# State reads of a gated delta-rule kernel on Trainium2: 64 columns in place of 128, with an overlapped layernorm, later loads and a loop body of four chunks

## The chip, the cores and the metric

The kernel is one program on one core of one Trainium2 chip. The metric is the device time of one launch in microseconds (us). TensorE (PE) runs its matmuls at one of two clock levels, 1.2 and 2.4 GHz; the profile writes the granted clock as 0.50 and 1.00 of full speed.

## The reference, cut to what matters

```python
xn = _layernorm(x, axis=-1)                      # x: (4, 512, 256)
def step(S, xs):                                 # per batch and head: 64 states S of 128x128
    q_t, k_t, v_t, a_t, b_t = xs
    Sk = einsum('bhvk,bhk->bhv', S, k_t)
    S = a_t[..., None] * S - (b_t[..., None] * (Sk - v_t))[..., None] * k_t[:, :, None, :]
    o_t = einsum('bhvk,bhk->bhv', S, q_t)
    return (S, o_t)
...
o = (o - mu) * lax.rsqrt(var + 1e-05) * ln_g + ln_b
return (o * g).reshape(B_, T_, H * DV) @ Wo.T
...
x = x + attention(xn) + ffn(xn)                  # ffn: router over 8 experts (top 2), LoRA on gate, up, down
```

q, k and v come from projections of xn, a causal convolution of four taps and a silu; the decays a and the weights beta come from sigmoids.

## The kernel before, in words

The five engines run hand-written queues; semaphores tie them together, and each engine takes its own queue in order. All tiles lie in one SBUF tile, `arena`, so nearly every row of the profile says arena; PSUM is `PS`, eight banks of 512 columns.

**Prelude (0 to 271 us).** x arrives in four quarters of 512 tokens. For each quarter VectorE (DVE) makes the layernorm in seven steps (lines 882 to 894: sum, mean, subtract, square, sum, reciprocal, multiply), with a square root on ScalarE (ACT, line 600) between them. TensorE transposes the quarter (line 1211), ACT copies it out (605, 608). When all four are done, TensorE computes the router logits (line 1219: 16 tiles of tokens, weights 128x128, 8 moving columns each), the beta projection (1225) and, after a chain of small DVE steps on the logits (909 to 927), transposes of the expert weights (1229). Then the FFN runs.

**Projections (271 to 740 us)** write q and k, k times beta, v, decays and suffix products to DRAM (`kq_d`, `kb_d`, `vas_d`, `e_d`), the last stores by SyncE's queue (SPq, lines 368 to 386).

**Start of the recurrence (738 to 790 us).** ACT issues the loads of the first two chunks (lines 700 to 702: KB, KQ, EX for chunk 0 and chunk 1), computes the first products, issues the loads of VAS (line 738, four slots), writes products to `r_d` and gathers them into `g_d` (732, 743), waits for the projections' stores, loads GB (748) and gives `x_read` (752), on which DVE's first step of chunk 0 (line 1051) waits.

**Recurrence (782 to about 2250 us).** 16 chunks of 32 tokens, each in 8 blocks (m) of 4 tokens, on 64 pairs of batch and head at once. DVE does the steps inside a block (1051 to 1074), takes off corrections from PSUM (1002, 1013), copies the block's last column of P (line 1114, the mark of a block's end used below), adds state updates (1019), extends decays (1025, 1030). TensorE turns P (1406) and makes the corrections (1418, 1335, weights of 32 rows). Beside that, in the blocks of `READ_AT`, it reads the states for the next chunk: 16 slots of 4 pairs per chunk. For a slot ACT scales four states (769), TensorE transposes them (1367), ACT copies them to `STR` (774), TensorE multiplies them with the next chunk's keys and queries (1379, `reads_of`), ACT copies the result into X (783). PSUM bank 6 holds the transposes and bank 7 the reads, one slot at a time. In between stand the update products (1393), the products for the next chunk (1303, 1325, `prep`), key transposes (1295) and, at the head of a chunk, three matmuls whose result nobody reads (1447, `keep_awake`).

A read multiplies each transposed state with the columns of two neighbouring pairs, its own and the other of the couple, 128 columns; the copy takes the half that belongs to its own pair:

```python
p0 = 4 * (g0 + gi) + j // 2 * 2
ins = mm(bank(7)[:, 128 * gi:128 * (gi + 1)]..., STR[:, s % 2, gi, :], KQ[d][:, :, p0:p0 + 2]...)
...
nc.scalar.copy(dst, bank(7).rearrange("v (g l o x) -> v o g l x", g=4, l=NB, o=2)[:, j % 2])
```

15 of the 16 chunks read, so there are 240 slots and 960 read matmuls; an fp32 matmul stands in the profile as two instructions, hence 1920. `chunks` runs the chunks in a loop whose body holds two of them (7 turns, chunks 0 to 13) and then chunks 14 and 15 alone.

**End (2250 to 2591 us).** Normalisation, gates and the output projection.

Of the kernel before, what the change touches and what calls it, by code (L numbers as in the profile page):

```python
# [28 lines left out]
HALO = KC - 1  # L29
# [70 lines left out]
def build(nc, x_tm, wqT, wkT, wvT, waT, wgT, woT, small, w_gate, w_up, w_down, a_gate, b_gate,  # L100
# [15 lines left out]
    with ExitStack() as ctx:  # L116
# [109 lines left out]
        XAG = take(CH)  # L226
        XAU = take(CH)
        SG = take(2 * CH).rearrange("p (s t) -> p s t", s=2)
        SQ = SG.rearrange("p s t -> p (s t)")
# [19 lines left out]
        ln_step, ln_var, ln_std, xn_ready = sem("ln_step"), sem("ln_var"), sem("ln_std"), sem("xn_ready")  # L249
# [345 lines left out]
        def _(act):  # L595

            act.wait_ge(consts, 7)
            for c in range(4):
# [3 lines left out]
                if c > 0:  # L602
                    for k in range(2):
                        act.wait_ge(xnT_psum, 2 * (c - 1) + k + 1)
                        nc.scalar.copy(XNT[:, k, c - 1, HALO:HALO + T], bank(2 * (c - 1) + k)).then_inc(xnT_ready, 1)
            for k in range(2):
                act.wait_ge(xnT_psum, 6 + k + 1)
                nc.scalar.copy(XNT[:, k, 3, HALO:HALO + T], bank(6 + k)).then_inc(xnT_ready, 1)
            act.wait_ge(logits, 1)
# [89 lines left out]
            for n in range(2):  # L699
                act.dma_start(KB[n].rearrange("k p t -> k (p t)"), kb_d[n:n + 1].rearrange("s k x -> k (s x)")).then_inc(kb_in[n], 16)  # L700
                act.dma_start(KQf[n], kq_d[n:n + 1].rearrange("s k x -> k (s x)")).then_inc(kq_in[n], 16)
                act.dma_start(EX[n].rearrange("v r p -> v (r p)"), e_d[n:n + 1].rearrange("s v x -> v (s x)")).then_inc(e_in[n], 16)

# [33 lines left out]
            for m in range(4):  # L737
                act.dma_start(VAS[:, m].rearrange("v r p t -> v (r p t)"), vas_d[:, m:m + 1].rearrange("v l r x -> v (l r x)")).then_inc(vas_in[m], 16)
# [21 lines left out]
            def chunk(n, i, c, nxt, nxt2):  # L760
# [15 lines left out]
                def read_copy(s):  # L776
# [6 lines left out]
                    nc.scalar.copy(dst, bank(7).rearrange("v (g l o x) -> v o g l x", g=4, l=NB, o=2)[:, j % 2]).then_inc(x_read, 1)  # L783
# [92 lines left out]
        def _(dve):  # L876
            tt = nc.vector.tensor_tensor

            for c in range(4):
                cs = slice(4 * c, 4 * c + 4)  # L880
                dve.wait_ge(ld_x[c], 16)
                nc.vector.tensor_reduce(ST8[:, 0, cs], XIN[:, cs, :], AX.X, ALU.add).then_inc(ln_step, 1)
                dve.wait_ge(ln_step, 5 * c + 1)
                nc.vector.tensor_scalar(ST8[:, 3, cs], ST8[:, 0, cs], -1.0 / D, None, ALU.mult).then_inc(ln_step, 1)
                dve.wait_ge(ln_step, 5 * c + 2)
                tt(XN[:, cs, :], XIN[:, cs, :], ST8[:, 3, cs].unsqueeze(2).to_broadcast([128, 4, D]), ALU.add).then_inc(ln_step, 1)
                dve.wait_ge(ln_step, 5 * c + 3)
# [315 lines left out]
        def _(pe):  # L1203
# [3 lines left out]
            for c in range(4):  # L1207
# [5 lines left out]

            pe.wait_ge(ld_small, 16)
            pe.wait_ge(xnT_ready, 8)
            for i in range(NX):
                at = HALO + 128 * (i % 4)
                for k in range(2):
                    ins = mm(bank(0)[:, E * i:E * (i + 1)], XNT[:, k, i // 4, at:at + 128], WR[:, k, :], start=(k == 0), stop=(k == 1))
            ins.then_inc(logits, 1)  # L1220
# [137 lines left out]
            def chunk(n, i, c, nxt, nxt2):  # L1358
# [11 lines left out]
                def reads_of(s):  # L1370
# [218 lines left out]
```

## Time and profile before

| | |
|---|---|
| median of 3 runs | 2592.14 us (2591.98 to 2592.34) |
| the profiled execution's own time | 2592.64 us |
| its span, first to last instruction | 2590.9 us |
| TensorE matmul busy | 2181.5 us (84%) |
| VectorE busy | 1925.3 us (74%) |
| ScalarE busy | 1276.5 us (49%) |
| mean granted TensorE clock | 0.912 |

The profiled execution's time is its span plus 1.7 us around it, and 0.5 us above the median of the runs. Busy shares are means over stages of different kinds, so stages and blocks are looked at one by one.

### The profile page before, as it was taken

What the parts mean: (1) busy time and instruction counts of PE and PEld (TensorE: products, weight loads), DVE (VectorE), ACT (ScalarE), POOL (GpSimd) and SP (SyncE); (2) the same over time, 40 slices, a digit from 0 to 9 for tenths busy, and PEclk for the clock granted to TensorE, in tenths of its full rate; (3) what the DMA queues carried; (4) which work ended last, traced back from release to release, by engine and by line L of the source; (5) the groups of instructions that cost most, each with busy time, mean ns of one, the idle gap of its engine ahead of it and who ended that gap; (6) DMA issues with size and microseconds to landing.
All of it is one profiled execution on the core that took longest, in us unless ns stands there. A gap on an engine that the chain in (4) does not pass through costs nothing.

```text
span 2590.9 us, 61369 instructions
## 1 busy us (share of the span) xinstructions
PE 2181.5 (84%) x21482; PEld 1606.6 (62%) x21482; DVE 1925.3 (74%) x4379; ACT 1276.5 (49%) x2731; POOL 578.6 (22%) x577
## 2 busy tenths in 40 slices
PE   5999999999948777778878878777878786799998
PEld 3444888888836666667666667666666665344343
DVE  5222799999968889888888888988887898633334
ACT  2000677777833555445445455554544543334443
POOL 0000244444442222122222222221222222200000
PEclk9999999999977898898898898888888988899999
DMA  6000277777684555555555555555555556310210
GB/s 244 8 8 8 101 277 266 266 265 268 237 328 148 200 180 196 165 189 183 170 196 176 182 176 183 202 166 190 184 165 196 178 193 216 144 66 16 81 67 23
DMA packets 211170, 434.65 MB, mean 168 GB/s; under 512 B 47153, under 2 KB 160553, under 8 KB 181721
## 3 DMA queue, kind: packets, MB, share of 16 engines
q1 hardware_dynamic: 207880, 420.24, 46.9%
q10 hardware_dynamic: 2976, 10.72, 1.0%
q8 instruction: 167, 2.74, 0.4%
q14 instruction: 99, 0.80, 0.1%
q0 software_dynamic: 48, 0.16, 0.0%
HBM read 295.13 MB, written 136.98 MB: 167 GB/s over the span
## 4 chain that ended last, share of the span: by engine, by line
PE 51%; DVE 22%; issue 13%; ACT 11%; SPq 1%; DVEq 1%; DMA 1%; ACTq 0%; POOL 0%; POOLq 0%
PE PS L1379 10%; DVE arena L968 8%; ACT arena L769 4%; PE PS L1520 4%; PE PS L1275 4%; PE PS L1325 3%; PE PS L1252 3%; PE PS L1418 3%; PE PS L1354 3%; PE PS L1367 3%; PE PS L1406 3%; DVE arena L1059 2%; DVE arena L1002 2%; PE PS L1506 2%; PE PS L1393 2%
## 5 line engine op out<-in xcount | busy, mean ns | idle before, releaser
L1275 PE MATMUL PS<-arena 128*128 x2048 | 463.6, 386 | 1.8 <-DVEq L953 0.9
L968 DVE SCALAR_TENSOR_TENSOR arena<-PS,SM,arena 128x256 f32<-128x256 f32 x1152 | 452.8, 474 | 15.5 <-ACT arena L648 15.5
L1275 PEld LDWEIGHTS PS<-arena 128*128 128x128 f32 x2048 | 383.4, 188 | 82.1 <-DVE arena L968 6.5
L1379 PE MATMUL PS<-arena 128*128 128x128 f32 x1920 | 332.3, 326 | 76.5 <-ACT arena L774 75.3
L1379 PEld LDWEIGHTS PS<-arena 128*128 128x128 f32 x1920 | 281.3, 225 | 119.4 <-ACT arena L774 93.7
L575 POOL TENSOR_TENSOR arena<-arena 128x256 f32<-128x256 f32 x128 | 114.7, 896 | 1062.2 <-DVE arena L1074 1062.2
L769 ACT ACTIVATE arena<-arena 128x128 f32<-128x128 f32 x960 | 302.0, 395 | 0.0
L648 ACT ACTIVATE arena<-PS,SM 128x256 f32<-128x256 f32 x384 | 209.8, 565 | 88.9 <-PE PS L1275 84.1
L783 ACT COPY arena<-PS 128x256 f32<-128x256 f32 x240 | 89.6, 373 | 267.1 <-PE PS L1379 266.2
L795 ACT COPY arena<-PS 128x512 f32<-128x512 f32 (+1 forms) x188 | 91.0, 520 | 263.0 <-PE PS L1406 262.7
L1367 PE MATMUL PS<-ident,arena 128*128 128x128 f32 x960 | 177.4, 316 | 27.0 <-ACT arena L769 25.2
L1393 PE MATMUL PS<-arena 32*128 32x128 f32 x1920 | 169.1, 324 | 31.8 <-issue 18.4
L1013 DVE TENSOR_TENSOR arena<-arena,PS 128x512 f32<-128x512 f32 x192 | 127.4, 684 | 86.8 <-PE PS L1418 84.4
L1051 DVE TENSOR_TENSOR arena<-arena 128x64 f32<-128x64 f32 x512 | 155.2, 303 | 43.1 <-issue 17.5
L1074 DVE TENSOR_TENSOR arena<-arena 128x384 f32<-128x384 f32 (+2 forms) x384 | 175.2, 456 | 13.8 <-DVE arena L1051 3.2
L543 POOL TENSOR_TENSOR arena<-arena 128x512 f32<-128x512 f32 x64 | 80.2, 1275 | 450.1 <-ACT arena L677 450.1
L1067 DVE TENSOR_TENSOR arena<-arena 128x384 f32<-128x384 f32 (+2 forms) x384 | 172.7, 450 | 6.6
L1059 DVE TENSOR_TENSOR arena<-arena 128x384 f32<-128x384 f32 (+2 forms) x384 | 173.8, 453 | 2.2
L1393 PEld LDWEIGHTS PS<-arena 32*128 32x128 f32 x1920 | 141.9, 221 | 53.4 <-issue 38.8
L1181 DVE TENSOR_TENSOR arena<-PS,arena 128x512 f32<-128x512 f32 x64 | 44.3, 692 | 171.9 <-ACT arena L854 171.9
L1418 PE MATMUL PS<-arena 32*128 32x64 f32 x3072 | 119.8, 289 | 59.2 <-ACT arena L795 59.2
L1367 PEld LDWEIGHTS PS<-ident,arena 128*128 128x128 f32 x960 | 130.1, 163 | 40.9 <-ACT arena L769 39.7
(135 smaller groups left out, 3549.5 us busy)
## 6 DMA issues: line engine op xcount, KB each, us to landing
arena<-g_d SPq DMA_DIRECT2D x126, 1024.0 KB, 5.1
arena<-vas_d SPq DMA_DIRECT2D x124, 384.0 KB, 3.3
vas_d<-arena SPq DMA_DIRECT2D x32, 1024.0 KB, 11.4
kq_d<-arena SPq DMA_DIRECT2D x8, 4096.0 KB, 11.5
arena<-kq_d SPq DMA_DIRECT2D x14, 2048.0 KB, 8.4
arena<-beta_d SPq DMA_DIRECT2D x8, 2048.0 KB, 9.1
kb_d<-arena SPq DMA_DIRECT2D x8, 2048.0 KB, 10.3
vas_d<-arena SPq DMA_DIRECT2D x8, 2048.0 KB, 12.4
```

The source lines that it names most:

```text
L648: nc.scalar.activation(ACC[:, x % NACC, h], raw[:, :, HALO:HALO + PT_], ACT.Identity, bias=CB[:, w, hh:hh + 1], scale=CW[:, w, KC - 1, hh: ...
L769: ins = nc.scalar.mul(S[:, p, :], S[:, p, :], EX[c][:, 6, p:p + 1])
L968: nc.vector.scalar_tensor_tensor(acc, raw[:, :, i:i + PT_], CW[:, w, i, hh:hh + 1], acc, ALU.mult, ALU.add).then_inc(job_free if i == TAPS ...
L1051: tt(W[:, :, t], V[:, :, t], W[:, :, t], ALU.add).then_inc(v_add, 1)
L1059: tt(xs, xs, A[:, :, t].unsqueeze(2).unsqueeze(3).to_broadcast([128, NP, 2, 3 - t]), ALU.mult).then_inc(x_dec, 1)
L1067: tt(TMP[:, :, 0:6 - 2 * t].rearrange("v p (e t) -> v p e t", e=2), GB[:, m % 2, :, t, :, t + 1:4], W[:, :, t].unsqueeze(2).unsqueeze(3).t ...
L1074: tt(xs, xs, TMP[:, :, 0:6 - 2 * t].rearrange("v p (e t) -> v p e t", e=2), ALU.subtract).then_inc(x_sub, 1)
L1275: ins = mm(dst.rearrange("p (b n) -> p b n", b=B), W4[:, w, kt, DH * h:DH * (h + 1)], XNT[:, kt, :, bass.ds(c * PT_ + (HALO - halo), halo ...
L1367: ins = nc.tensor.transpose(bank(6)[:, 128 * gi:128 * (gi + 1)], S[:, 4 * (g0 + gi) + j, :], ident[:, :])
L1379: ins = mm(bank(7)[:, 128 * gi:128 * (gi + 1)].rearrange("v (l x) -> v l x", l=NB), STR[:, s % 2, gi, :], KQ[d][:, :, p0:p0 + 2].rearrange ...
L1393: ins = mm(bank(4 + b)[:, 128 * gi:128 * (gi + 1)], PT32[rows, g0 + gi, :], KBT[rows, g0 + gi, :], start=True, stop=True)
L1418: ins = mm(bank(j)[:, 64 * g:64 * (g + 1)], PTL[rows, 128 * g:128 * (g + 1)], GL[L][rows, 64 * (s * G + g):64 * (s * G + g + 1)], start=Tr ...
```

## The change

Four edits. The reads multiply the 64 columns of their own pair alone, into 64 columns of bank 7 each, and the copy takes 256 columns that lie side by side. The layernorm's squares move from DVE to ACT, subtraction and multiplication become one DVE instruction per tile of tokens, the four quarters overlap, and the router's matmuls of a quarter stand between the transposes of later quarters. On ACT's queue at the start of the recurrence, the loads of chunk 1's KB, KQ and EX and of three of the four VAS slots move behind the loads of GB. The loop over chunks has a body of four chunks (3 turns) and the last four chunks stand alone.

```diff
         def chunks(engine, chunk):
-            with engine.Fori(0, NS // 2 - 1) as i:
-                for c in range(2):
-                    chunk(i * 2 + c, i, c, True, True)
+            with engine.Fori(0, NS // 4 - 1) as i:
+                for q in range(4):
+                    chunk(i * 4 + q, i * 2 + q // 2, q % 2, True, True)
+            for c in range(2):
+                chunk(NS - 4 + c, NS // 2 - 2, c, True, True)
...
-            for n in range(2):
+            def load_keys(n):
                 act.dma_start(KB[n]...); act.dma_start(KQf[n]...); act.dma_start(EX[n]...)
+            def load_values(m):
+                act.dma_start(VAS[:, m]...)
+            load_keys(0)
...
-            for m in range(4):
-                act.dma_start(VAS[:, m]...)
+            load_values(0)
...  (r_d, g_d, waits for the stores, GB)
+            load_values(1)
+            load_keys(1)
+            for m in range(2, 4):
+                load_values(m)
             act.wait_ge(zeros, 5)
             nc.scalar.nop().then_inc(x_read, 1)
...
-                    nc.scalar.copy(dst, bank(7).rearrange("v (g l o x) -> v o g l x", g=4, l=NB, o=2)[:, j % 2]).then_inc(x_read, 1)
+                    nc.scalar.copy(dst, bank(7, 256).rearrange("v (g l x) -> v g l x", g=4, l=NB)).then_inc(x_read, 1)
...
+            def mean(c):
+                ...  # sum, times -1/D
+            def variance(c):
+                dve.wait_ge(ln_sq, c + 1)
+                nc.vector.tensor_reduce(ST8[:, 1, 4 * c:4 * c + 4], SQ[c % 2], AX.X, ALU.add).then_inc(ln_var, 1)
+            def normalise(c):
+                ...  # reciprocal
+                for n in range(4 * c, 4 * c + 4):
+                    ins = nc.vector.tensor_scalar(XN[:, n, :], XIN[:, n, :], ST8[:, 3, n:n + 1], ST8[:, 4, n:n + 1], ALU.add, ALU.mult)
...
+            transposes(0)
+            for c in range(1, 4):
+                transposes(c)
+                router(c - 1)
+            router(3)
...
                     for gi in range(4):
-                        p0 = 4 * (g0 + gi) + j // 2 * 2
-                        ins = mm(bank(7)[:, 128 * gi:128 * (gi + 1)].rearrange("v (l x) -> v l x", l=NB), STR[:, s % 2, gi, :],
-                                 KQ[d][:, :, p0:p0 + 2].rearrange("k l p e t -> k l (p e t)"), start=True, stop=True)
+                        ins = mm(bank(7)[:, 64 * gi:64 * (gi + 1)].rearrange("v (l x) -> v l x", l=NB), STR[:, s % 2, gi, :],
+                                 KQ[d][:, :, 4 * (g0 + gi) + j].rearrange("k l e t -> k l (e t)"), start=True, stop=True)
```

TensorE's queue in the prelude, before (1211 are the transposes, 1219 the router):

```order
L1211 MATMUL PS<-ident,arena 128x128 x7
L1211 MATMUL PS<-ident,arena 128x128 [waits xn_ready]
L1211 MATMUL PS<-ident,arena 128x128 x7
L1211 MATMUL PS<-ident,arena 128x128 [waits xn_ready]
L1211 MATMUL PS<-ident,arena 128x128 x7
L1219 MATMUL PS<-SM,arena 128x8 [waits xnT_ready,ld_small]
L1219 MATMUL PS<-SM,arena 128x8 x31
```

and in the changed kernel, where the transposes are line 1256 and the router 1265:

```order
L1256 MATMUL PS<-ident,arena 128x128 [waits xn_ready]
L1256 MATMUL PS<-ident,arena 128x128 x7
L1265 MATMUL PS<-SM,arena 128x8 [waits xnT_ready]
L1265 MATMUL PS<-SM,arena 128x8 x7
L1256 MATMUL PS<-ident,arena 128x128 [waits xn_ready]
L1256 MATMUL PS<-ident,arena 128x128 x7
L1265 MATMUL PS<-SM,arena 128x8 [waits xnT_ready]
L1265 MATMUL PS<-SM,arena 128x8 x7
L1265 MATMUL PS<-SM,arena 128x8 [waits xnT_ready]
L1265 MATMUL PS<-SM,arena 128x8 x7
```

Each quarter's eight router matmuls now stand behind the next quarter's transposes, and only the last eight are left behind the last transposes.

ACT's transfers at the start of the recurrence, before:

```order
L700 DMA arena<-kb_d 128x2048
L701 DMA arena<-kq_d 128x4096
L702 DMA arena<-e_d 128x448
L732 DMA r_d<-arena 32x512 x4
...
L738 DMA arena<-vas_d 128x768 x4
L743 DMA g_d<-r_d 8x32x8 x4
L748 DMA arena<-g_d 128x2048 x2
```

and in the changed kernel (723 to 725 are KB, KQ and EX, 728 VAS, 775 GB):

```order
L728 DMA arena<-vas_d 128x768
L770 DMA g_d<-r_d 8x32x8 x4
L775 DMA arena<-g_d 128x2048 x2
L728 DMA arena<-vas_d 128x768
L723 DMA arena<-kb_d 128x2048
L724 DMA arena<-kq_d 128x4096
L725 DMA arena<-e_d 128x448
L728 DMA arena<-vas_d 128x768 x2
```

Chunk 1's three loads and three of the four VAS loads now stand behind GB, ahead of the instruction that gives `x_read`.

TensorE's queue in the first read block of a chunk, before (1379 is the read):

```order
L1367 MATMUL PS<-ident,arena 128x128 x4
L1388 REGISTER_ALU
L1393 MATMUL PS<-arena 128x128 x8
L1374 ISA
L1379 MATMUL PS<-arena 128x128 x4
L1367 MATMUL PS<-ident,arena 128x128 x4
```

and in the changed kernel (1431 is the read):

```order
L1420 MATMUL PS<-ident,arena 128x128 x4
L1440 REGISTER_ALU
L1445 MATMUL PS<-arena 128x128 x8
L1427 ISA
L1431 MATMUL PS<-arena 128x64 x4
L1420 MATMUL PS<-ident,arena 128x128 x4
```

Nothing moved here; the number of read matmuls stays and their columns are halved.

## Rows read from the trace of the kernel before

**Rows 1.** The page: busy time of the engines, share of the span, instructions.
```profile
PE 2181.5 (84%) x21482; PEld 1606.6 (62%) x21482; DVE 1925.3 (74%) x4379; ACT 1276.5 (49%) x2731; POOL 578.6 (22%) x577
```

**Rows 2.** Busy time by engine in stretches: PE, PEld, DVE, ACT, POOL; clock, DMA, GB/s.
```profile
738.00:782.00 44.00, 6.86 (x228) 6.22 (x232) 13.52 (x10) 5.25 (x6) 14.54 (x12) 0.56 0.94 339
866.00:2165.00 1299.00, 1029.60 (x16192) 859.58 (x16192) 1113.95 (x2564) 663.67 (x1695) 314.02 (x339) 0.87 0.54 182
```

**Rows 3.** The page: the chain that ended last, by engine.
```profile
PE 51%; DVE 22%; issue 13%; ACT 11%; SPq 1%; DVEq 1%; DMA 1%; ACTq 0%; POOL 0%; POOLq 0%
PE PS L1379 10%; DVE arena L968 8%; ACT arena L769 4%; PE PS L1520 4%; PE PS L1275 4%; PE PS L1325 3%; PE PS L1252 3%; PE PS L1418 3%; PE PS L1354 3%; PE PS L1367 3%; PE PS L1406 3%; DVE arena L1059 2%; DVE arena L1002 2%; PE PS L1506 2%; PE PS L1393 2%
```

**Rows 4.** Groups by line and form: line, engine, tiles, count; busy us, mean ns; idle before.
```profile
L1379 PE MATMUL PS<-arena 128*128 128x128 f32 x1920 | 332.3, 326 | 76.5 <-ACT arena L774 75.3
L783 ACT COPY arena<-PS 128x256 f32<-128x256 f32 x240 | 89.6, 373 | 267.1 <-PE PS L1379 266.2
L658 ACT ACTIVATE arena<-PS,BAH 128x256 f32<-128x256 f32 x128 | 53.1, 469 | 0.0
L1187 DVE TENSOR_SCALAR arena<-arena,SM 128x512 f32<-128x512 f32 x64 | 34.5, 539 | 0.4
```

**Rows 5.** Timeline: one slot's read at either clock, the router, projections of 268 columns.
```profile
1391.68 2.08 PE L1379 MATMUL PS<-arena 128*128 128x128 f32 x8 [0.68 <-ACT arena L774]
...
1323.41 1.16 PE L1379 MATMUL PS<-arena 128*128 128x128 f32 x8 [1.44 <-ACT arena L774]
...
36.71 13.79 PE L1219 MATMUL PS<-SM,arena 128*128 128x8 f32 x64 [0.77 <-ACT arena L608]
...
727.62 8.26 PE L1275 MATMUL PS<-arena 128*128 x36
```

**Rows 6.** Busy time by engine in stretches of the recurrence, columns as in rows 2.
```profile
1388.40:1402.00 13.60, 12.42 (x82) 10.55 (x85) 10.25 (x23) 6.67 (x17) 2.61 (x4) 0.50 0.67 244
1402.00:1424.00 22.00, 16.91 (x282) 14.33 (x274) 18.27 (x40) 14.04 (x37) 4.81 (x6) 1.00 0.51 163
```

**Rows 7.** The same view, from one block's end (line 1114) to a later one.
```profile
1298.79:1331.86 33.07, 24.91 (x351) 21.25 (x349) 29.01 (x64) 20.57 (x55) 7.43 (x9) 0.95 0.61 208
1388.64:1424.70 36.06, 29.10 (x352) 24.64 (x350) 28.98 (x65) 21.12 (x55) 7.42 (x9) 0.81 0.56 191
...
1181.81:1191.43 9.62, 7.77 (x95) 6.62 (x95) 9.30 (x22) 5.57 (x15) 2.35 (x3) 0.82 0.47 128
1276.09:1285.69 9.60, 8.31 (x85) 7.02 (x86) 9.29 (x22) 5.09 (x13) 2.34 (x3) 0.66 0.53 166
```

**Rows 8.** Timeline of the prelude: one quarter's steps, and its last transposes.
```profile
4.86 1.22 DVE L882 TENSOR_REDUCE arena<-arena 128x4 f32<-128x1024 f32 x1 [4.86 <-DMA arena<-x_tm]
6.11 0.17 DVE L884 TENSOR_SCALAR arena<-arena 128x4 f32<-128x4 f32 x1
...
10.14 1.28 ACT L600 ACT_TABLE_LOAD   x1 [10.14 <-DVE arena L890]
11.43 0.30 ACT L600 ACTIVATE arena<-arena,eps 128x4 f32<-128x4 f32 x1
...
33.98 1.97 PE L1211 MATMUL PS<-ident,arena 128*128 128x128 f32 x8 [4.94 <-DVE arena L894]
```

**Rows 9.** Timeline, start of the recurrence; the last number is what a wait ended on.
```profile
766.42 8.90 SPq L386 DMA_DIRECT2D e_d<-arena  x1
...
780.80 0.95 POOL L564 MEMSET arena<- 128x1024 f32 x1 [28.27 <-DMA e_d<-arena]
781.80 7.10 PE L1335 MATMUL PS<-arena 32*128 32x64 f32 x128 [15.27 <-POOL arena L564]
...
785.67 1.41 DVE L1002 TENSOR_TENSOR arena<-arena,PS 128x256 f32<-128x256 f32 x4 [3.30 <-PE PS L1335]
```

**Rows 10.** Timeline: TensorE behind a turn of the loop, and inside its body.
```profile
1157.39 2.08 PE L1393 MATMUL PS<-arena 32*128 32x128 f32 x16 [3.62 <-issue]
...
1247.51 1.36 PE L1393 MATMUL PS<-arena 32*128 32x128 f32 x16 [1.19 <-DVE arena L1002]
```

More of the change, by code:

```diff
@@ L225, in build @@
         WT = take(NT)
-        XAG = take(CH)
-        XAU = take(CH)
+        XAf = take(2 * CH)
+        XAG, XAU = XAf[:, 0:CH], XAf[:, CH:2 * CH]
         SG = take(2 * CH).rearrange("p (s t) -> p s t", s=2)
-        SQ = SG.rearrange("p s t -> p (s t)")
+        SQ = [x.rearrange("p (n d) -> p n d", n=4) for x in (SG.rearrange("p s t -> p (s t)"), XAf)]
         HAD = take(CH)
@@ L248, in build @@
         consts, masks = sem("consts"), sem("masks")
-        ln_step, ln_var, ln_std, xn_ready = sem("ln_step"), sem("ln_var"), sem("ln_std"), sem("xn_ready")
+        ln_sum, ln_mean, ln_sq, ln_var = sem("ln_sum"), sem("ln_mean"), sem("ln_sq"), sem("ln_var")
+        ln_std, ln_rec, xn_ready = sem("ln_std"), sem("ln_rec"), sem("xn_ready")
         xnT_psum, xnT_ready = sem("xnT_psum"), sem("xnT_ready")
@@ L597, in _, with squares, deviation @@
             act.wait_ge(consts, 7)
-            for c in range(4):
+            def squares(c):
+                act.wait_ge(ln_mean, c + 1)
+                if c >= 2:
+                    act.wait_ge(ln_var, c - 1)
+                for n in range(4):
+                    ins = nc.scalar.activation(SQ[c % 2][:, n], XIN[:, 4 * c + n, :], ACT.Square, bias=ST8[:, 3, 4 * c + n:4 * c + n + 1])
+                ins.then_inc(ln_sq, 1)
+            def deviation(c):
                 act.wait_ge(ln_var, c + 1)
@@ L601, in _, with transposed @@
                                      bias=eps[:, 0:1], scale=1.0 / D).then_inc(ln_std, 1)
[L602 to L609, printed above, removed]
+            def transposed(c):
+                for k in range(2):
+                    act.wait_ge(xnT_psum, 2 * c + k + 1)
+                    nc.scalar.copy(XNT[:, k, c, HALO:HALO + T], bank(2 * c + k)).then_inc(xnT_ready, 1)
+            squares(0)
+            squares(1)
+            deviation(0)
+            squares(2)
+            deviation(1)
+            transposed(0)
+            squares(3)
+            deviation(2)
+            transposed(1)
+            deviation(3)
+            transposed(2)
+            transposed(3)
+            act.wait_ge(logits, 4)
             nc.scalar.activation(SC[:, :, :], bank(0, 128).rearrange("p (n e) -> p n e", n=NX), ACT.Sigmoid).then_inc(scores, 1)
@@ new lines, in mean @@
+                nc.vector.tensor_reduce(ST8[:, 0, cs], XIN[:, cs, :], AX.X, ALU.add).then_inc(ln_sum, 1)
+                dve.wait_ge(ln_sum, c + 1)
+                nc.vector.tensor_scalar(ST8[:, 3, cs], ST8[:, 0, cs], -1.0 / D, None, ALU.mult).then_inc(ln_mean, 1)
+            def variance(c):
+                dve.wait_ge(ln_sq, c + 1)
+                nc.vector.tensor_reduce(ST8[:, 1, 4 * c:4 * c + 4], SQ[c % 2], AX.X, ALU.add).then_inc(ln_var, 1)
+            def normalise(c):
+                cs = slice(4 * c, 4 * c + 4)
+                dve.wait_ge(ln_std, c + 1)
+                nc.vector.reciprocal(ST8[:, 4, cs], ST8[:, 2, cs]).then_inc(ln_rec, 1)
+                dve.wait_ge(ln_rec, c + 1)
+                for n in range(4 * c, 4 * c + 4):
+                    ins = nc.vector.tensor_scalar(XN[:, n, :], XIN[:, n, :], ST8[:, 3, n:n + 1], ST8[:, 4, n:n + 1], ALU.add, ALU.mult)
+                ins.then_inc(xn_ready, 1)
@@ L896, in _ @@
+            mean(0)
+            mean(1)
+            variance(0)
+            for c in range(4):
+                if c < 2:
+                    mean(c + 2)
+                normalise(c)
+                if c < 3:
+                    variance(c + 1)
             dve.wait_ge(consts, 9)
@@ L1205, in _, with transposes @@
             pe.wait_ge(consts, 9)
-            for c in range(4):
+            def transposes(c):
                 pe.wait_ge(xn_ready, c + 1)
@@ L1212, in _, with router @@
                     ins.then_inc(xnT_psum, 1)
-            pe.wait_ge(ld_small, 16)
[L1215 to L1220, printed above, removed]
+            def router(c):
+                pe.wait_ge(xnT_ready, 2 * c + 2)
+                for i in range(4 * c, 4 * c + 4):
+                    at = HALO + 128 * (i % 4)
+                    for k in range(2):
+                        ins = mm(bank(0)[:, E * i:E * (i + 1)], XNT[:, k, c, at:at + 128], WR[:, k, :], start=(k == 0), stop=(k == 1))
+                ins.then_inc(logits, 1)
+            pe.wait_ge(ld_small, 16)
+            transposes(0)
[3 more added lines that the diff above has]
+            router(3)
             for b in range(B):
```

15 lines of the change are left out of this document (1 added, 14 removed).

## The prediction

> **What bounds the kernel now.** I read the page first: TensorE is busy for 84% of the span, DVE for 74% [rows 1]. That is a mean over unlike stages, so the view by stretches comes next. The chain of waits lies on TensorE for 51% and on DVE for 22%, and its longest line is the read itself, L1379, with 10% of the span [rows 3], about 260 of the 332.3 us for which that line is busy [rows 4]. So TensorE and DVE are both close to the bound: DVE has work for 86% of a chunk, and TensorE, whose queue is in order, delays the corrections that DVE waits for whenever the reads run long. The reads matter, and so does the clock at which everything beside them runs.
>
> **1. The reads' own time.** A slot's read is eight instructions: 2.08 us at half speed, 1.16 us at full speed [rows 5]. Does the number of moving columns set this? The router says no: 64 instructions with weights as wide as those of the reads, but 8 columns in place of 128, took 13.79 us [rows 5], 0.215 us each. The reads at half speed come every 0.22 to 0.26 us (2.08 / 8 is 0.26 with the run-out of the last one). That the router ran at half speed too is read from its spacing; it can't be less than that of the same loads at full speed, 1.16 / 8 = 0.145. So the 128x128 weights, loaded anew for each matmul, set the pace, and the columns stream beneath them. What 64 columns save is the run-out of a slot's last matmul: the projections stream 268 columns in 8.26 / 36 = 0.229 us at full speed [rows 5], 0.86 ns a column, so 0.055 us at full and 0.11 at half speed. ACT's copy waits for exactly that end: 266.2 us of waiting over 240 slots [rows 4]. 240 x 0.055 to 0.11 is 13 to 26 us, of which three quarters lie on the chain (260 / 332): **-14 us**. The bounds: 0, and, if the weight loads did not count and the columns did, half of the reads, 332.3 / 2 x 3/4 = -125. I take the low end because the router's row has the same weights. The copy still moves 256 elements per row, so its 373 ns stay [rows 4].
>
> The Trainium skill ("TensorE: Matmul & The Clock Gate", section Back-to-back issue gap) gives an isolated matmul's spacing as proportional to its columns, about 60 cycles up to 64 columns against 134 at 128; by that the reads would halve and the sum would be that of rival 2. The router's row speaks against it.
>
> **2. The clock.** Take two stretches of the recurrence [rows 6]. In 1388 to 1402 us TensorE is busy for 12.42 of 13.60 us (91%), and the clock is 0.50; in 1402 to 1424 it is busy for 16.91 of 22.00 (77%), and the clock is 1.00. Being busy does not keep the clock up. The router shows the same: 13.79 us without a gap, weights loading all the time, and the pace stays that of half speed [rows 5]. What these have in common is little streamed through the array per microsecond: 8 columns per weight load, or weights that fill a quarter of it (L1393, L1418). The reads are the largest full-width work of the recurrence: 1920 x 128 columns, against 960 x 128 for the state transposes. Half of their columns go, and nothing takes their place; their time stays, since the weight loads set it. So I expect the clock to fall in read blocks that now keep it.
>
> The price of that is in the trace, because chunks differ in their clock for the same work. The last three read blocks (ends of blocks 4 to 7) took 33.07 us at 0.95 and 36.06 us at 0.81, with the same 29.0 us of DVE work [rows 7]. Time at half speed was 2 x 0.05 x 33.07 = 3.3 against 2 x 0.19 x 36.06 = 13.7 us: 2.99 us for 10.4, or 0.29 us per us. The block before block 3's end cost nothing: 9.62 at 0.82, 9.60 at 0.66 [rows 7]; there DVE hides it (9.3 of 9.6 us busy). I take the blocks that end at 2, 4, 5, 6 and 7, some 56 us of a chunk, of which about 9 are at half speed already, so 47 can be lost. How many will be is what I can't read from a row. I take two fifths, 19 us: a halving of the reads takes a good part of what is streamed there, but the transposes, the key transposes and the three idle matmuls at the head of a chunk stay. 19 x 0.29 = 5.5 us a chunk, in 15 chunks **+83 us**. Bounds: 0, and all 47 us, +204; below zero is excluded, since nothing streams more than before.
>
> **3. The prelude.** One quarter costs DVE two reductions of 1.22, three passes of about 1.23 and small steps of about 0.17 us, with a wait for ACT's root [rows 8]; the last transposes run from 33.98 to 35.95 us [rows 8], the router from 36.71 to 50.50 [rows 5]. After the change DVE has two reductions (2.44), two small steps (0.35) and four TENSOR_SCALAR of 256 elements (539 ns for 512 [rows 4], so some 0.3 each): 4.0 us a quarter. ACT gets four squares of 256 elements (at most 0.47 each [rows 4]) and one more table load (1.28 [rows 8]); that is under DVE's time. TensorE is then the limit: it can start at about 14 us (first sum at 4.86, squares and two table loads to 12.6, normalise to 14) and needs 4 x 1.97 + 13.79 = 21.7 us, so the logits stand at about 36 in place of 50.5. All that follows depends on them: **-14 us**, -10 to -16. The queue of SyncE isn't touched.
>
> **4. The loads.** From 738 to 782 us the DMA engines are 94% busy [rows 2], and chunk 0 waits for the store of `e_d`, issued at 766.42 and landed when POOL goes on at 780.80 [rows 9]. The loads moved behind GB are 1.0 + 2.0 + 0.2 MB and three times 0.4 MB: 4.4 MB, 13 us at the 339 GB/s of that stretch [rows 2]. The store can land some 10 us sooner, since part of that traffic lies beside its own. Against that, six more transfers are issued by ACT ahead of `x_read`, about 4 us, of which 3.30 are covered by DVE's wait for the first carried products [rows 9]. Chunk 1's keys are first read in block 1, some 20 us later, so they land in time. **-7 us**, -11 to +3.
>
> **5. The loop.** Behind a turn TensorE starts its first updates after 3.62 us of idle time put down to issue, inside the body after 1.19 [rows 10]. Most of the 2.4 us lies beside DVE's corrections; I count 0.5 for each of the four turns that go: **-2 us**, 0 to -4 (0 if that idle time has another cause than the turn).
>
> **The sum**, against the profiled execution's 2592.64 us (0.5 above the median): 2592.64 - 14 + 83 - 14 - 7 - 2 = 2638.6, so **2639 us**, slower by 1.8%.
>
> **The rivals.**
> *Rival 1: the clock holds.* The reads still stand back to back, and the clock level stays as it is wherever it is now. Then 2592.64 - 37 = **2556 us**, faster. It decides below 37 / (15 x 0.29) = 8.5 us of added half-speed time per chunk; that is a mean clock of 0.82 in the loop. For it: the reads are about a third of the full-width columns, so half of them is a sixth; against it, the stretch at 0.50 with TensorE 91% busy [rows 6]. The Trainium skill ("TensorE: Matmul & The Clock Gate", section Loop structure matters more than you think) holds that matmuls back to back stay at the high clock and that waits lose it; by that rule the clock would hold and this rival's time would come out. The stretch just named disagrees with it.
> *Rival 2: the reads halve.* If the columns set the pace, the reads save 125 in place of 14 us: 2592.64 - 125 - 23 = **2445 us** with the clock as now. Against it stands the router's row.
> *Rival 3: a small fall.* The clock drops in a few blocks only, and the price eats the other gains: 5 to 12 us of half speed a chunk, +22 to +52, so 2578 to 2608 us, centred on no change.
> That the edit does nothing at all to TensorE is excluded by the order, which shows 64 columns in place of 128; the prelude and the loads do what they say in any case.
>
> **How the numbers follow.** A measurement of this kernel can tell 0.2%, 5.2 us, from no change. Forecast (2608 us and above): 0.68. Rival 1: 0.13. Rival 2: 0.03. Rival 3: 0.16, of which a bit under half falls within 0.2%, most of the rest below. So slower 0.70, same 0.06, faster 0.24. The range leaves out rival 2, most of rival 1, and the top of the clock's bounds: above 2710 us nearly 35 of the 47 us would have to go. **2560 to 2710 us**; the forecast's own range is 2608 to 2710.
>
> **What would show it.** Router done near 36 us; the store of `e_d` landed near 770; a slot's read still above 1.0 us at full and about 2.0 at half speed; the loop's clock at 0.75 to 0.80 in place of 0.87, chunks of 96 to 98 us in place of 92, and DVE waiting longer for L1418's successor. Wrong if the clock stays at 0.85 or more, or if a read takes 0.7 us.

## The result, and the profile after

The changed kernel takes **2791.64 us** (median of 4 runs, 2785.23 to 2810.02) against 2592.06 us for the kernel before on the same chip: ratio 1.0775, 95% interval 1.0755 to 1.0794. The forecast was 2639 us with a range up to 2710: the sign was right, the size was not. The profiled execution took 2785.23 us, 192.6 more than the profiled one of before.

The page: busy time of the engines, and the chain that ended last by engine and by line.

```profile
PE 2455.0 (88%) x21482; PEld 1859.6 (67%) x21482; DVE 1913.5 (69%) x4383; ACT 1295.3 (47%) x2748; POOL 569.9 (20%) x577
...
PE 60%; DVE 19%; issue 11%; ACT 8%; DMA 1%; DVEq 1%; ACTq 1%; POOL 0%; POOLq 0%; SPq 0%
PE PS L1431 12%; DVE arena L1013 9%; PE PS L1420 5%; PE PS L1378 5%; PE PS L1458 4%; PE PS L1445 4%; PE PS L1572 4%; PE PS L1470 4%; PE PS L1388 3%; PE PS L1305 3%; PE PS L1407 3%; ACT arena L800 2%; PE PS L1328 2%; PE PS L1558 2%; DVE arena L1104 2%
```

TensorE has as many instructions as before and is busy 273.5 us longer [rows 1]; DVE is busy 12 us less. TensorE's share of the chain has grown from 51% to 60%, DVE's and ACT's have shrunk [rows 3]. Where in the program, the view by stretches tells: 14 chunks, from the end of chunk 0 to the end of chunk 14, of the kernel before, and then of the changed one (length; busy us of PE, PEld, DVE, ACT, POOL; clock; DMA).

```profile
871.85:2161.32 1289.47, 1022.02 (x16100) 853.04 (x16100) 1107.41 (x2548) 657.38 (x1681) 311.66 (x336) 0.87 0.55 182
```

```profile
860.19:2347.23 1487.04, 1272.98 (x16101) 1085.93 (x16101) 1105.15 (x2549) 667.30 (x1680) 304.01 (x336) 0.68 0.47 158
```

A chunk takes 1487.04 / 14 = 106.2 us in place of 92.1. The clock is 0.68 in place of 0.87: time at half speed is 2 x 0.32 x 106.2 = 68 us of a chunk in place of 2 x 0.13 x 92.1 = 24. These 14 chunks are 197.6 us longer, about the whole difference; most of what the start gained (below; the first block ends 23.8 us earlier) was lost again in chunks 0 and 15 (12.1 and 6.6 us).

The reads (L1431, L1379 before), the copy that waits for them, and a DVE line that waits for the corrections, by line and form:

```profile
L1431 PE MATMUL PS<-arena 128*128 128x64 f32 x1920 | 401.7, 378 | 49.2 <-ACT arena L805 48.9
...
L1058 DVE TENSOR_TENSOR arena<-arena,PS 128x512 f32<-128x512 f32 x192 | 127.5, 685 | 180.9 <-PE PS L1470 178.7
...
L814 ACT COPY arena<-PS 128x256 f32<-128x256 f32 x240 | 89.6, 373 | 340.1 <-PE PS L1431 340.1
```

and that DVE line in the kernel before:

```profile
L1013 DVE TENSOR_TENSOR arena<-arena,PS 128x512 f32<-128x512 f32 x192 | 127.4, 684 | 86.8 <-PE PS L1418 84.4
```

With half the columns the reads are busy for 401.7 us in place of 332.3, ACT waits 340 us for them in place of 266 [rows 4], and DVE 178.7 us for the corrections in place of 84.4. The timeline of TensorE shows why (the stretch into block 5; in brackets the idle time before):

```profile
1453.29 1.10 PE L1431 MATMUL PS<-arena 128*128 128x64 f32 x8
1454.23 0.61 PE L1420 MATMUL PS<-ident,arena 128*128 128x128 f32 x4
1457.57 1.45 PE L1356 MATMUL PS<-arena 128*32 128x64 f32 x64 [2.73 <-DVE arena L1058]
1458.95 1.97 PE L1431 MATMUL PS<-arena 128*128 128x64 f32 x8
...
1462.45 1.97 PE L1431 MATMUL PS<-arena 128*128 128x64 f32 x8 [0.68 <-ACT arena L805]
...
1467.53 2.08 PE L1445 MATMUL PS<-arena 32*128 32x128 f32 x16
1469.54 1.97 PE L1431 MATMUL PS<-arena 128*128 128x64 f32 x8
```

A slot's read takes 1.10 us at full and 1.97 at half speed: 0.05 and 0.1 us less than before [rows 5], no more. But 141 of the 240 slots run at half speed from end to end, where 45 did before. Behind a wait of 2.73 us all that follows runs at half speed, for some 17 us, though no idle time of TensorE in it is above 0.7 us.

The other parts of the change do what they should. The router of the first quarter, the transposes of the last, and the rest of the router:

```profile
19.82 3.42 PE L1265 MATMUL PS<-SM,arena 128*128 128x8 f32 x16
...
28.11 1.95 PE L1256 MATMUL PS<-ident,arena 128*128 128x128 f32 x8
29.85 6.83 PE L1265 MATMUL PS<-SM,arena 128*128 128x8 f32 x32
```

It is done at 36.7 us in place of 50.5 [rows 5]. At the start of the recurrence:

```profile
742.82 6.06 SPq L389 DMA_DIRECT2D e_d<-arena  x1
753.44 0.95 POOL L567 MEMSET arena<- 128x1024 f32 x1 [14.68 <-DMA e_d<-arena]
755.07 7.10 PE L1388 MATMUL PS<-arena 32*128 32x64 f32 x128 [0.89 <-DVE arena L1021]
762.23 0.28 DVE L1096 TENSOR_TENSOR arena<-arena 128x64 f32<-128x64 f32 x1 [7.31 <-ACTq L783]
```

The store of `e_d` has landed at 753.44 in place of 780.80, and the carried products begin at 755.07 in place of 781.80 [rows 9]: 13.8 us of these 27 come from the prelude (the projections end at 722.1 us in place of 735.9), the other 13 from the loads. Some 3 of them go again, since DVE now waits 7.31 us for the issue of the loads on ACT's queue (3.30 for the carried products before).

### The profile page after: what moved, and what is told of

Same layout as the page of the kernel before. It is cut to its first block, busy times and chain, and to the rows that moved or that the text cites. A ratio compares the mean times of both kernels' runs of the same rounds, so it can differ in the third digit from the quotient of the medians.

```text
span 2783.5 us, 60812 instructions
## 1 busy us (share of the span) xinstructions
PE 2455.0 (88%) x21482; PEld 1859.6 (67%) x21482; DVE 1913.5 (69%) x4383; ACT 1295.3 (47%) x2748; POOL 569.9 (20%) x577
## 4 chain that ended last, share of the span: by engine, by line
PE 60%; DVE 19%; issue 11%; ACT 8%; DMA 1%; DVEq 1%; ACTq 1%; POOL 0%; POOLq 0%; SPq 0%
PE PS L1431 12%; DVE arena L1013 9%; PE PS L1420 5%; PE PS L1378 5%; PE PS L1458 4%; PE PS L1445 4%; PE PS L1572 4%; PE PS L1470 4%; PE PS L1388 3%; PE PS L1305 3%; PE PS L1407 3%; ACT arena L800 2%; PE PS L1328 2%; PE PS L1558 2%; DVE arena L1104 2%
## 5 line engine op out<-in xcount | busy, mean ns | idle before, releaser
L1013 DVE SCALAR_TENSOR_TENSOR arena<-PS,SM,arena 128x256 f32<-128x256 f32 x1152 | 452.8, 478 | 15.5 <-ACT arena L670 15.5
L1431 PE MATMUL PS<-arena 128*128 128x64 f32 x1920 | 401.7, 378 | 49.2 <-ACT arena L805 48.9
L1328 PEld LDWEIGHTS PS<-arena 128*128 128x128 f32 x2048 | 383.4, 188 | 82.1 <-DVE arena L1013 6.5
L1431 PEld LDWEIGHTS PS<-arena 128*128 128x128 f32 x1920 | 360.9, 281 | 96.2 <-ACT arena L805 69.9
L1058 DVE TENSOR_TENSOR arena<-arena,PS 128x512 f32<-128x512 f32 x192 | 127.5, 685 | 180.9 <-PE PS L1470 178.7
L1420 PE MATMUL PS<-ident,arena 128*128 128x128 f32 x960 | 215.6, 367 | 16.6 <-ACT arena L800 14.5
L1445 PE MATMUL PS<-arena 32*128 32x128 f32 x1920 | 191.1, 355 | 12.8 <-DVE arena L1047 8.0
L1458 PE MATMUL PS<-ident,arena 128*128 128x128 f32 x624 | 133.7, 367 | 73.7 <-DVE arena L1159 35.3
L1445 PEld LDWEIGHTS PS<-arena 32*128 32x128 f32 x1920 | 163.0, 251 | 38.9 <-issue 30.2
L1470 PE MATMUL PS<-arena 32*128 32x64 f32 x3072 | 133.5, 313 | 58.5 <-ACT arena L826 58.5
L1420 PEld LDWEIGHTS PS<-ident,arena 128*128 128x128 f32 x960 | 158.4, 202 | 31.1 <-ACT arena L800 28.6
L1378 PE MATMUL PS<-arena 128*32 128x64 f32 x5120 | 153.3, 308 | 27.1 <-DMA arena<-kq_d 18.5
```

The costliest lines, as they stand in the source:

```text
L1013: nc.vector.scalar_tensor_tensor(acc, raw[:, :, i:i + PT_], CW[:, w, i, hh:hh + 1], acc, ALU.mult, ALU.add).then_inc(job_free if i == TAPS ...
L1328: ins = mm(dst.rearrange("p (b n) -> p b n", b=B), W4[:, w, kt, DH * h:DH * (h + 1)], XNT[:, kt, :, bass.ds(c * PT_ + (HALO - halo), halo ...
L1378: ins = mm(bank(bk)[32 * j:32 * j + 32, to:to + 64].rearrange("r (l x) -> r l x", l=nl), PTL[:, at:at + 32], KQ[c][:, l0:l0 + nl, p0:p0 + ...
L1420: ins = nc.tensor.transpose(bank(6)[:, 128 * gi:128 * (gi + 1)], S[:, 4 * (g0 + gi) + j, :], ident[:, :])
L1431: ins = mm(bank(7)[:, 64 * gi:64 * (gi + 1)].rearrange("v (l x) -> v l x", l=NB), STR[:, s % 2, gi, :], KQ[d][:, :, 4 * (g0 + gi) + j].rea ...
L1445: ins = mm(bank(4 + b)[:, 128 * gi:128 * (gi + 1)], PT32[rows, g0 + gi, :], KBT[rows, g0 + gi, :], start=True, stop=True)
```

## The experiments

Each run stands beside the kernel before, which took 2592 to 2594 us in all of them. "A stretch" is the time from one block's end on DVE to the next, and its means are over chunks 1 to 14, from the trace, with half-speed time from the granted clock. In the changed kernel the stretches into blocks 0 to 7 are at half speed for 16.1, 6.8, 7.3, 6.9, 4.5, 13.4, 7.2 and 6.7 us (before: 4.5, 3.9, 1.4, 6.3, 0.4, 5.7, 1.3, 0.2). The expectations of e5 and later give some such times up to 1.3 us otherwise (12.8 for this 13.4, 1.4 for the 2.7 us of e1's stretch into block 5): there the clock's record is laid 1.5 us off the instructions. Where it stands, it fits the pace of the changed kernel's reads and transposes throughout: 0.11 us from one instruction to the next at full speed, 0.21 at half speed.

### Is it the reads?

**e1**, against the changed kernel (the copy back to a half of 128 columns as well):

```
-  mm(bank(7)[:, 64 * gi:64 * (gi + 1)]..., STR[...], KQ[d][:, :, 4 * (g0 + gi) + j]...)
+  p0 = 4 * (g0 + gi) + j // 2 * 2
+  mm(bank(7)[:, 128 * gi:128 * (gi + 1)]..., STR[...], KQ[d][:, :, p0:p0 + 2]...)
```

> The changed kernel with the reads alone put back to the 128 columns of two pairs; the layernorm, the loads and the loop body stay changed. Clock theory (halving the read columns is the whole loss): the loop's clock returns to about 0.87, chunks to about 92 us, half-speed time per chunk from 69 to about 24 us, and the time to 2592 - 14 (layernorm) - 10 (loads) - 2 (loop) = about 2566 us. Rival A (one of the joined edits, the body of four chunks or the order of the loads, shifts the phases and costs the clock): the clock stays near 0.67 and the time near 2790 us.

Measured: **2571.57 us** (2564.11 to 2578.85), ratio 0.992 (0.9902 to 0.9938), faster than both kernels. **e2** is the reverse: the kernel before, with the narrow reads alone.

> The kernel before with the reads alone narrowed to 64 columns. Clock theory: the loss of the changed kernel without its gains, 2792 + 26 = about 2818 us, loop clock about 0.67, chunks of about 106 us. Rival A: 2592 less the run-out of the reads, 14 us, so about 2578 us at a clock of 0.87.

Measured: **2845.33 us**, ratio 1.0986 (1.0921 to 1.1051), 27 us above what was expected: the narrow reads cost 251 us in this kernel and 220 in the changed one. **e3** takes the own pair and half of its neighbour (`[:, :, lo:lo + 12]` of the two pairs' 16, `lo = 4 * (j % 2)`).

> The changed kernel with reads of 96 columns: the own pair and half of its neighbour. Clock theory, if the loss grows evenly with the columns taken away: half of it, so half-speed time of about 46 us per chunk and about 2680 us; if the clock falls from a point on, one of the two ends, 2566 or 2790 us. Rival B (something in the narrow form other than its columns, such as the copy or the layout of the bank, is slow): the layout with 96 is new as well, so about 2790 us at whatever clock.

Measured: **2619.58 us**, ratio 1.0088 (1.0071 to 1.0105). **e4** puts the lost columns back as idle work:

```
-  pe.wait_ge(tr_ready, n * 16 + s + 1)
   ...  (the wait for kq_in or x_read, as it was)
+  mm(bank(7)[:, 256:512]..., ident, ident.unsqueeze(1).to_broadcast([128, 2, 128]))
+  pe.wait_ge(tr_ready, n * 16 + s + 1)
```

> The changed kernel, reads of 64 columns, with one idle matmul of 256 columns per slot ahead of the reads, while TensorE waits for ACT's copy of the states; its result is used by nothing. It streams as many columns as the reads have lost (two instructions of 256 against eight times 64). Clock theory: the loop's clock comes back to 0.85 or more, half-speed time to 30 us a chunk or less, and the chunk falls from 106 us by some 10 us, less what of the idle matmuls' 16 x 0.44 = 7 us lies on the path: 2570 to 2680 us. Rival B (the narrow reads cost by another way than the columns streamed): the clock stays near 0.67 and the added work makes it slower, 2790 to 2900 us.

Measured: **2655.73 us**, ratio 1.0237 (1.022 to 1.0255). The 14 chunks in e1, e2, e3 and e4, in the view by stretches:

```profile
849.17:2132.73 1283.56, 1020.88 (x16100) 851.97 (x16100) 1111.89 (x2548) 657.28 (x1682) 312.22 (x336) 0.87 0.54 183
```

```profile
879.91:2413.74 1533.83, 1317.76 (x16102) 1125.95 (x16102) 1101.28 (x2548) 667.54 (x1680) 303.97 (x336) 0.64 0.46 153
```

```profile
853.65:2192.07 1338.42, 1091.88 (x16100) 915.16 (x16100) 1110.10 (x2549) 660.61 (x1682) 311.38 (x336) 0.80 0.53 175
```

```profile
856.42:2221.88 1365.46, 1166.64 (x16548) 962.53 (x16548) 1106.78 (x2549) 657.42 (x1681) 300.96 (x336) 0.84 0.52 172
```

The clock comes and goes with the columns streamed: 0.87 with 128, 0.80 with 96, 0.68 and 0.64 with 64. The joined edits are cleared (rival A). Idle columns bring back 0.84 and 136 us, although TensorE does more work: the narrow form itself is not slow (rival B). The idle matmuls of e4 fill waits as well, so that run alone can't tell columns from waits; e1 and e3, which change nothing but the reads' columns and their copy, can. And the loss is not in proportion: the first 32 columns cost 48 us, the next 32 cost 172. With 96 columns a read takes 1.13 us at full speed, half way between 1.16 and 1.10, but of the stretches one has turned, the one into block 5: 13.97 us, all of it at half speed in all 14 chunks, against 10.57 with 2.7 us in e1. That is 3.40 of the 3.9 us by which the chunk is longer; into block 4 half speed grew by 2.8 us, for 0.45 us of length.

### How half speed is handed on

**e5** gives 128 columns to slots 14 and 15 alone, the last reads of a chunk.

> The changed kernel with the reads of slots 14 and 15 alone (the last two of a chunk, ahead of the carried products) at 128 columns, the other fourteen at 64. Theory C (the half speed of the block into 0 is inherited: it begins in the narrow reads of block 7 and the transposes and carried products behind them, whose weights fill a quarter of the array, never end it): the block into 0 goes back from 20.2 to about 14.8 us, its half-speed time from 17 to about 4 us, the other blocks stay; 15 x 5.4 = 81 us less, about 2710 us. Rival D (the carried products bring the half speed about themselves, whatever stands ahead): block 0 stays at 20 us and the time at 2785 to 2790 us.

Measured: **2719.89 us**, ratio 1.0532 (1.0482 to 1.0581): 72 us of the loss from 2 of 16 slots, as theory C had it. The stretch into block 0 took 15.5 us on average, 6.4 at half speed, in place of 20.25 with 16.1. First one such stretch of the changed kernel in the view by stretches, then one of e5, which holds the same DVE work:

```profile
1391.70:1412.58 20.88, 18.71 (x174) 15.10 (x174) 10.60 (x31) 3.37 (x7) 2.30 (x3) 0.55 0.41 139
```

```profile
1359.27:1375.21 15.94, 13.79 (x172) 9.57 (x171) 10.86 (x32) 2.91 (x6) 2.30 (x3) 0.79 0.50 181
```

TensorE's timeline there, the changed kernel first, then e5: last read, transposes of P32, carried products.

```profile
1391.43 1.97 PE L1431 MATMUL PS<-arena 128*128 128x64 f32 x8
1394.42 3.67 PE L1458 MATMUL PS<-ident,arena 128*128 128x128 f32 x16 [1.03 <-ACT arena L752]
1398.03 7.11 PE L1388 MATMUL PS<-arena 32*128 32x64 f32 x128
```

```profile
1355.49 2.08 PE L1438 MATMUL PS<-arena 128*128 128x128 f32 x8
...
1358.76 1.16 PE L1438 MATMUL PS<-arena 128*128 128x128 f32 x8 [0.24 <-ACT arena L806]
1360.94 1.96 PE L1468 MATMUL PS<-ident,arena 128*128 128x128 f32 x16 [1.02 <-ACT arena L753]
1362.83 2.90 PE L1393 MATMUL PS<-arena 32*128 32x64 f32 x95
```

The narrow reads leave the clock low; the transposes take 3.67 in place of 1.96 us, and the carried products, whose weights fill 32 rows, do not raise it: 7.11 us for 128 instructions. In e5 slot 14 runs at half speed, slot 15 at full, and what follows inherits that: in 12 of the 14 chunks these 128 instructions take 3.80 us.

**e6** and **e9** were meant for the stretch into block 5.

> The changed kernel with the reads of slots 9 and 10 alone (block 5) at 128 columns. With 96 columns in all slots this block alone stayed at half speed from end to end. If a block's clock is set by its own reads: block 5 goes from 13.4 to about 10.6 us, the others stay, 15 x 2.8 = 42 us less, about 2749 us; if what is won is also handed on to blocks 6 and 7, up to 5.8 us a chunk, 2705 us. If the block enters at half speed and two wide reads can't lift it: 2785 to 2790 us.

> The run with slots 9 and 10 wide, and besides two idle matmuls of 512 columns in the wait of 2.7 us at block 5's head. There the clock fell while TensorE waited, and the two wide reads behind it ran at half speed. If that wait is what lets block 5 fall: block 5 goes from 13.2 to about 11 us, its half-speed time from 11.6 to under 4 us, 15 x 2 = 30 us less than the 2760 us of that run, about 2730 us. If block 5 falls whatever fills the wait: block 5 at 13 us or more, 2760 us plus up to 15 us for the idle matmuls.

Measured: e6 **2760.2 us** (1.0629, 1.0602 to 1.0655), e9 **2782.16 us** (1.0724, 1.0707 to 1.0742). Both were put into the wrong place: by the timeline slots 9 and 10 run a stretch later, and the idle matmuls of e9 stood behind the wait. Read for where they are, the wide reads of e6 help their own stretch: into block 6 it takes 11.86 us in place of 13.03 with 3.2 us at half speed in place of 7.2, while the one into block 5 keeps its 13.2. **e12** widens slots 7 and 8, which do run there.

> The changed kernel with the reads of slots 7 and 8 at 128 columns, the others at 64. By the timeline these two, and not slots 9 and 10, run between the ends of blocks 4 and 5, behind the wait of 2.7 us. If a block's clock hangs on its own reads: that stretch goes from 13.4 to about 10.7 us, its half-speed time from 12.8 to under 4 us, 15 x 2.7 = 41 us less, about 2750 us. If the wait in front of slot 8's reads alone makes it fall and two wide reads can't lift it: no change, 2785 to 2795 us.

Measured: median **2746.23 us**, but the four runs lie between 2700 and 2773, too far apart for a verdict on the time, so I read the stretch alone: into block 5 11.89 us with 5.1 at half speed, in place of 13.41 with all of it. Its own reads lift it, one slot late: slot 7 still runs at half speed. **e13** and **e15** leave all reads narrow and put the same two matmuls into the stretch, e13 at slot 8, e15 at slot 7:

```
   state_transposes(s)
+  if s == 7:
+      pe.wait_ge(x_read, 1 + n * 16 + s)
+      for _ in range(2):
+          mm(bank(7)..., ident, ident.unsqueeze(1).to_broadcast([128, 4, 128]))
```

> The changed kernel, all reads of 64 columns, with two idle matmuls of 512 columns in the wait of 2.7 us ahead of slot 8's reads, where the run before it meant to put them. If the wait makes the stretch into block 5 fall: its half-speed time goes from 12.8 to under 4 us, 13.4 to about 11.2 us, 15 x 2.2 = 33 us less, about 2759 us. If it falls whatever fills the wait: 13.4 us or more, 2790 to 2815 us.

> The changed kernel, all reads of 64 columns, with two idle matmuls of 512 columns between slot 7's state transposes and the key products, where the timeline shows the wait of 2.7 us; the earlier runs had put them one slot or more too late. If the wait makes the stretch into block 5 fall: its half-speed time from 12.8 to under 4 us, 13.4 to about 10.8 us, 15 x 2.6 = 39 us less, about 2753 us. If the narrow reads behind it fall by themselves: 13 us or more, 2785 to 2800 us.

Measured: e13 **2810.77 us** (1.0851, 1.082 to 1.0883), 19 us slower than without; e15 **2739.43 us** (1.0556, 1.0539 to 1.0574), 52 us faster. Their timelines, e13 first:

```profile
1462.96 1.36 PE L1356 MATMUL PS<-arena 128*32 128x64 f32 x64 [2.71 <-DVE arena L1058]
1464.25 1.97 PE L1431 MATMUL PS<-arena 128*128 128x64 f32 x8
1466.02 1.06 PE L1420 MATMUL PS<-ident,arena 128*128 128x128 f32 x4
1466.87 3.62 PE L1517 MATMUL PS<-ident 128*128 128x512 f32 x4
1470.29 1.09 PE L1431 MATMUL PS<-arena 128*128 128x64 f32 x8
```

```profile
1438.69 1.98 PE L1517 MATMUL PS<-ident 128*128 128x512 f32 x4
1441.39 1.10 PE L1356 MATMUL PS<-arena 128*32 128x64 f32 x64 [0.72 <-DVE arena L1058]
1442.42 1.10 PE L1431 MATMUL PS<-arena 128*128 128x64 f32 x8
...
1444.64 1.10 PE L1431 MATMUL PS<-arena 128*128 128x64 f32 x8 [0.68 <-ACT arena L805]
```

In e13 they run behind the wait, at half speed, 3.62 us, and the clock is high for what follows, but the stretch is longer (14.46 us with 9.8 at half). In e15 they run inside the wait in 1.98 us, and the fall comes later: 10.32 us with 4.4 at half, as short as in e1. The wait and the narrow columns act together, but the narrow columns are not needed for the fall. In the kernel before the same stretch, with 128-column reads behind the same wait, falls whole in 4 of 14 chunks (one is the first stretch of [rows 6]); in e1 it falls whole in none, as in this chunk:

```profile
1365.42:1375.72 10.30, 7.77 (x85) 6.47 (x87) 9.82 (x22) 6.28 (x17) 2.34 (x3) 0.89 0.82 315
```

With 96 or 64 columns in all slots (e3, e2 and the changed kernel) it falls whole in 14 of 14, with the wait filled (e15) in none. Whether the filling acts by ending the idle time or by its own 2048 columns, no run tells apart.

### The other edits, and a faster kernel

> The kernel of 128-column reads with the joined edits (2571.6 us), with the loads in their old order. If the loads gave what the trace of the start shows: the end of chunk 0's first block moves from 772.9 to about 783 us, and the time is 10 us more, about 2582 us. If that gain came with the prelude: no move, 2572 us.

> The kernel of 128-column reads with the joined edits (2571.6 us), with the loop's body of two chunks. If a turn costs what the idle time at it suggests: four turns more, 0.5 us each on the path, 2 us more, 2574 us, not to be told from no change. If the body of four chunks costs or gains by another way (the clock's phases): over 10 us either way.

Both are e1 with one edit undone. e10: **2577.6 us** (2574.88 to 2582.16), 6 us above e1, ratio to before 0.9945 (0.9929 to 0.9962); chunk 0's first block ends at 781.0 in place of 772.9 us, since the store lands later:

```profile
765.49 0.95 POOL L567 MEMSET arena<- 128x1024 f32 x1 [26.76 <-DMA e_d<-arena]
```

That row stands at 753.74 in e1, 11.8 us earlier. The loads are worth 8 us at that place; the 6 us at the end are not clear of the noise, since the two intervals overlap. e11: **2570.49 us** (2570.10 to 2571.62), 0.9912 (0.9895 to 0.9928): the loop's body can't be told from no change.

Could idle columns lift what half speed is left in e1? **e7** has `keep_awake(5)` in place of 3, **e8** two more idle groups, **e14** and **e16** (on e11's kernel) the two matmuls of e13 and of e15.

> The kernel of 128-column reads with the joined edits (2571.6 us), with five idle matmuls in place of three at the head of a chunk; the two more fit the 2.07 us for which TensorE waits there. If columns streamed hold the clock: the half speed of block 1 and of the start of block 2 (5.7 and 2.9 us a chunk) shrinks, block 2 from 11.85 to about 10.9 us, 15 x 0.9 = 14 us less, about 2558 us. If the idle matmuls run at half speed themselves and delay the transposes behind them: 2572 to 2590 us.

> As the run with five idle matmuls at the head, and besides one of 512 columns in front of block 3's transposes (a wait of 1.25 us) and two in block 5 (a wait of 2.68 us). If columns streamed in waits hold the clock: block 4 (1.7 us at half speed), block 5 and the start of block 6 (1.4 and 2.6 us) come to nearly full speed too, another 5 us of half speed a chunk at 0.29, 15 x 1.5 = 22 us less, about 2536 us. If they delay what waits behind them: 2560 to 2590 us.

> The kernel of 128-column reads with the layernorm and the loads changed and the loop's body of two (2570.5 us), with the same two idle matmuls in the wait of 2.7 us. There the stretches into blocks 5 and 6 are at half speed for 4.5 and 2.7 us a chunk. If the wait starts that: both shrink, 11.3 to about 10.6 and 11.6 to 11.2 us, 15 x 1.0 = 15 us less, about 2555 us. If not: 2570 to 2597 us.

> The kernel of 128-column reads with the layernorm and the loads changed and the body of two (2570.5 us), with the same two idle matmuls in that wait. If the wait starts what half speed is left in the stretches into blocks 5 and 6 (4.5 and 2.7 us a chunk): 11.3 to about 10.6 and 11.6 to 11.2 us, 15 us less, about 2555 us. If not: 2570 to 2597 us.

Measured: e7 **2586.47 us** (0.9968, 0.9951 to 0.9984), e8 **2591.01 us** (0.9992, 0.9977 to 1.0007), e14 **2594.85 us** (1.001, 0.9997 to 1.0022): all slower than e1. In e7 the half speed into block 1 shrinks as expected (4.2 us, 6.6 in e1), but that stretch gets no shorter (9.19 us, 8.83 in e1); neither does the one that should have gained (into block 2 11.97 us, 11.85 in e1), the one into block 5 is at half speed for 5.9 us in place of 2.7, and the chunk is 2.2 us longer (in e7's slowest run against e1's fastest; the medians lie 15 us apart). The further groups of e8, like those of e14, stood behind the waits they were meant for. In e8 half speed does fall, from 23.2 us a chunk in e1 to 20.5, and still the chunk is 1.8 us longer: the clock alone does not set the time. e16: **2567.78 us** (2566.74 to 2571.40), 0.9901 (0.9885 to 0.9918), the lowest median of all, but not to be told from e11: the stretch into block 5 goes from 11.34 to 10.30 us as expected (at half speed from end to end in none of 14 chunks, in 4 in e11), the one into block 6 grows from 11.58 to 12.41. With wide reads the gain of one stretch is lost in the next.

## Why the prediction was wrong

By its own steps:

1. *The reads' own time, -14 us*: right for a slot. 0.053 us less at full and 0.104 at half speed, against 0.055 and 0.11. Rival 2 is out: half the columns do not halve the reads. The sum of -14 us no run shows by itself.
2. *The clock, +83 us*: **the step that failed**, in its size. That the clock falls, and that the lost columns bring this about, is shown (e1 to e4). The price per microsecond was near: 0.29 was taken, and (106.2 - 92.1) / (68 - 24) is 0.32. Wrong was the sentence "I take two fifths, 19 us" of added half-speed time a chunk, and the choice of blocks behind it. It was 44 us. In the five stretches that I had chosen it was 30 us (8.9 to 39.0), and they became 8.5 us longer, not 5.5. And I left out the stretch into block 0, for whose block no read is listed. It lost most: 11.6 us more at half speed, 14.77 to 20.25 us, 5.5 of the 14.1 us a chunk. The state is handed on, and work with 32-row weights keeps it where the reads left it (e5). The two fifths came from no row, as the prediction says; it weighed what goes on streaming beside the reads, and e3 shows that the loss does not go by such a share: 48 us for the first quarter of the columns and 172 for the second. The narrow reads came to +220 us in all (e1), so with their -14 the clock to some +234, above the upper bound that I had named (all 47 us, +204).
3. *The prelude, -14 us*: right, the router ends 13.8 us earlier.
4. *The loads, -7 us*: 8 where they act; about 6 at the end, not clear of the noise (e10).
5. *The loop, -2 us*: can't be told from nothing (e11).

Without the reads the sum was -14 - 7 - 2 = -23 us; e1 stands 22.7 us below the kernel before, its runs within 15 us of each other. Of the signs that were named, the router's end and the reads' 1.10 and 1.97 us came. The clock (0.68) and the chunks (106.2 us) went beyond theirs, and the store landed at 753 and not near 770, a figure that left out the 14 us of the prelude.

The Trainium skill ("TensorE: Matmul & The Clock Gate", section Loop structure matters more than you think) has it that dense matmuls stay at the high clock and waits lose it. e15 and e16 agree on the waits: with 2.0 of the 2.7 us filled, the stretch into block 5 falls whole in no chunk. On dense work the trace differs: TensorE is busy for 1272.98 of 1487.04 us at 0.68, more than before at 0.87.

What stays open: why, with the same 128-column reads, that stretch falls whole in 4 of 14 chunks in the kernel before and in e11, and in none in e1; why in e16 the next stretch loses what this one gains; and in which stretch a given set of idle columns will be needed. Each of these has to be run.

## What to carry to other kernels

Dropping columns that nobody reads was not free here: the instructions take nearly as long as before (1.10 us a slot in place of 1.16), and TensorE lost its clock for much of what stands around them. Ask what the stretch streams at full width after the edit, and which narrow work behind it will inherit the lower clock. Here the three other edits with the 128-column reads kept are the better kernel, 0.992 of the time before.

## What was not expected of the hardware

A quarter of the reads' columns cost 48 us and half of them 220: the clock's loss came stretch by stretch, not evenly. With a quarter of the columns gone one stretch fell from end to end in every chunk; the one that lost most time, into block 0, fell only with half of them gone. Two matmuls whose results nothing uses, placed in a wait, made a kernel 52 us faster; one slot later in TensorE's queue, behind the wait, they made it 19 us slower. Between these two runs (e15, e13) the work is the same.
